# Layer 3's scales from bounds instead of measured maxima, in a four-layer graph kernel on one core

## What is computed

```python
v = causal_vars.at[:, intervention_idx].set(intervention_value)
for _ in range(MAX_STEPS):
    effects = jnp.einsum('nm,bmd->bnd', adj_matrix, v)
    h = jnp.concatenate([v, effects], axis=-1)
    h = jax.nn.relu(jnp.einsum('bnk,dk->bnd', h, W1) + b1)
    v = jnp.einsum('bnk,dk->bnd', h, W2) + b2
return v
```

## Time and profile before

| | us |
|---|---|
| three runs | 1045.5, 1045.57, 1046.95 |
| median | 1045.57 |
| the profiled execution's own time | 1046.92 |
| its span, first to last instruction | 1045.1 |
| PE busy in the span | 1024.1 |
| DVE busy | 692.9 |
| POOL busy | 534.7 |
| ACT busy | 453.1 |
| granted clock of TensorE, mean | 0.995 |

### The profile page before, as it was taken

How to read it: one execution, slowest core, us unless ns; L and a number is a source line. 1 busy time by engine, 2 the same in 40 slices (tenths; PEclk the granted TensorE clock), 3 DMA queues, 4 the chain that set the end, 5 groups by cost and what they waited for, 6 DMA issues and landing times.

```text
span 1045.1 us, 18762 instructions
## 1 busy us (share of the span) xinstructions
PE 1024.1 (98%) x6922; PEld 492.3 (47%) x6922; DVE 692.9 (66%) x1728; ACT 453.1 (43%) x1097; POOL 534.7 (51%) x625
## 2 busy tenths in 40 slices
PE   7999999999999999999999999999999999999995
PEld 3445444444444444434455555555554545455553
DVE  4877565656555886686577777875546676767556
ACT  4632323333334543444424667556557622141632
POOL 0005486644546686577645758579764233223311
PEclk9999999999999999999999999999999999999998
DMA  9930000000000000000010121112212100000022
GB/s 369 400 129 1 2 1 2 1 2 2 1 1 2 2 1 2 1 1 2 1 41 2 41 82 51 71 41 82 81 42 82 41 1 1 3 1 22 21 61 61
DMA packets 14658, 45.66 MB, mean 44 GB/s; under 512 B 960, under 2 KB 9280, under 8 KB 10080
## 3 DMA queue, kind: packets, MB, share of 16 engines
q1 hardware_dynamic: 14560, 44.39, 11.5%
HBM read 40.19 MB, written 4.19 MB: 42 GB/s over the span
## 4 chain that ended last, share of the span: by engine, by line
PE 95%; DVE 3%; ACT 1%; issue 0%; DMA 0%; SPq 0%; DVEq 0%; ACTq 0%
PE PS L771 37%; PE PS L901 23%; PE PS L945 18%; PE PS L823 5%; PE PS L756 2%; PE PS L758 2%; PE PS L757 2%; PE PS L765 1%; PE PS L764 1%; PE PS L763 1%; PE PS L746 1%; PE PS L926 1%; PE PS L747 1%; DVE X L1224 1%; DVE T L1224 0%; PE PS L809 0%
## 5 line engine op out<-in xcount | busy, mean ns | idle before, releaser
L771 PE MATMUL PS<-BW,S 128*128 128x512 fp8e4 x1792 | 403.2, 379 | 0.8 <-DVE R L1224 0.8
L771 PEld LDWEIGHTS PS<-BW,S 128*128 128x128 f16 x1792 | 169.9, 98 | 207.3 <-issue 16.6
L1064 ACT ACTIVATE T<-PS,SM 128x128 f32<-128x128 f32 x384 | 112.8, 365 | 234.5 <-DVE X L1224 157.2
L901 PE MATMUL PS<-WZ,R 64*128 64x512 f16 x1536 | 198.0, 377 | 1.7 <-ACT T L1064 1.7
L1768 POOL TENSOR_TENSOR T<-T 128x128 f32<-128x128 f32 (+1 forms) x192 | 124.3, 648 | 127.8 <-ACT T L1064 117.5
L1224 DVE SCALAR_TENSOR_TENSOR X<-PS,SM,X 128x128 f32<-128x128 f32 x320 | 110.0, 344 | 81.9 <-PE PS L901 81.9
L901 PEld LDWEIGHTS PS<-WZ,R 64*128 64x128 f16 x1536 | 69.5, 94 | 104.6 <-issue 26.3
L945 PE MATMUL PS<-BW,S 128*128 128x512 fp8e4 x512 | 115.4, 379 | 0.3 <-issue 0.3
L1224 DVE SCALAR_TENSOR_TENSOR T<-PS,SM,T 128x128 f32<-128x128 f32 x256 | 88.2, 344 | 28.9 <-PE PS L901 28.6
L1768 POOL TENSOR_TENSOR S<-R,S 128x512 f16<-128x512 f32 x48 | 57.5, 1210 | 93.5 <-ACT S L1064 93.5
L901 PE MATMUL PS<-WZ,T 64*128 64x512 f16 x768 | 103.8, 376 | 0.0
(11 more groups left out here) (215 smaller groups left out, 1480.0 us busy)
## 6 DMA issues: line engine op xcount, KB each, us to landing
WZ<-a_in SPq DMA_DIRECT2D x16, 1024.0 KB, 4.8
BW<-at_in SPq DMA_DIRECT2D x8, 1024.0 KB, 18.5
R<-at_in SPq DMA_DIRECT2D x7, 1024.0 KB, 12.4
out<-X SPq DMA_DIRECT2D x16, 256.0 KB, 2.3
X<-x_in SPq DMA_DIRECT2D x3, 1024.0 KB, 19.9
T<-w_in SPq DMA_DIRECT2D x1, 1536.0 KB, 15.4
R<-at_in SPq DMA_DIRECT2D x2, 512.0 KB, 4.8
SM<-sm_in SPq DMA_DIRECT2D x1, 520.5 KB, 18.0
```

What stands on the lines that cost most here:

```text
L771: m = e.matmul(o, stile(h, t, c), Bm[:, t, block(j)], start=(t == 0 and h == 0), stop=(last and t == NT - 1 and h == 1))
L901: m = e.matmul(bank(b0 + q), halves[kd][zh][r, :], WZ[r, wh, kd, block(g)], start=(i == 0), stop=(i == 8))
L1064: return e.activation(o, i, f, **kw)
```

## The change

The measured maxima go, with their semaphores and tiles. In `scales_b` the bound on the entries of pass 1's result is carried on to passes 2 and 3 by a factor `cNMG` (from column sums of the weights), and gives the scales of all three passes. The inverse, the scale and the factor `cKG` of each pass then stand there before layer 3 begins; `CR` becomes one row of 64 for each pass, written in step `rows`, and `rk` one row in place of two.

```diff
-    at(24, ("gmax", 1, 0))
-    at(25, ("gcol", 1, 0), ("step", 1, 0))
...
-        h, (p, g) = 14 * (n - 5), divmod(n - 2, 2)
-        on(h, ("gmax", p, g))
-        on(h + 2, ("gcol", p, g), ("step", p, g), *take(n, 0, "X11"))
+        h = 14 * (n - 5)
+        on(h + 2, *take(n, 0, "X11"))
...
-    for g in range(2):
-        on((29, 44)[g], ("fin", g))
+    on(29, ("fin",))
...
-        CR = flatR[:, 5248:5376].rearrange("p (k c) -> p k c", c=C)
-        rk = flatR[:, 5504:5536].rearrange("p (k t) -> p k t", t=NT)
+        CR = [flatR[:, k:k + C] for k in (5248, 5312, 5536)]
+        rk = flatR[:, 5504:5520]
...
-                elif kind == "gcol":
-                    p, g = step[1:]
-                    o = pe_aux(e, step)
-                    e.wait_ge(s_gmx, 2 * (p - 1) + g + 1)
-                    e.matmul(o[:, 0:128], gmh[:, g:g + 1].broadcast_to([128, 128]), i16[:, :], start=True,
-                             stop=True).then_inc(s_gmc, 1)
...
-                        fn(RT[k % 4], bank(product_bank(k)), ACT.Relu, scale=col(cKG0)).then_inc(s_gt, 1)
+                        fn(RT[k % 4], bank(product_bank(k)), ACT.Relu, scale=col(cKG + 1)).then_inc(s_gt, 1)
...
-                    p, g = divmod(n, 2)
+                    p = n // 2
                     e.wait_ge(s_p, slot_done(n, s, jj))
...
-                    e.wait_ge(s_kg, 2 * (p - 2) + g + 1)
                     o, i = RT[rt_buf(s, jj)], bank(pair_bank(n, s, jj))
                     if s == 6:
-                        fn(o, i, ACT.Relu, scale=col(cKG + g)).then_inc(s_gt, 1)
+                        fn(o, i, ACT.Relu, scale=col(cKG + p)).then_inc(s_gt, 1)
                     else:
-                        fn(o, i, ACT.Copy, scale=col(cKG + g)).then_inc(s_cp, 1)
+                        fn(o, i, ACT.Copy, scale=col(cKG + p)).then_inc(s_cp, 1)
...
-                    fn(RT[rt_buf(3, jj)], bank(aux_bank[step]), ACT.Copy, scale=col(cKG + n % 2)).then_inc(s_cp, 1)
+                    fn(RT[rt_buf(3, jj)], bank(aux_bank[step]), ACT.Copy, scale=col(cKG + n // 2)).then_inc(s_cp, 1)
...
-                fc(ts(e, col(cHB), col(cHB), 1e-10, qmax, ALU.max, ALU.mult))
-                fc(ts(e, col(cHB), col(cHB), 1.0 / 30000, None, ALU.mult))
-                fc(e.reciprocal(col(cT2), col(cHB)))
-                fc(ts(e, col(cKG0), col(cT2), col(cIRho), col(cT0), ALU.mult, ALU.mult))
-                fc(ts(e, cs[:, cSG:cSG + 4], ones[:, 0:4], col(cT2), None, ALU.mult))
-                fc(ts(e, cs[:, cISG:cISG + 4], ones[:, 0:4], col(cHB), None, ALU.mult))
+                fc(ts(e, col(cHB), col(cHB), 1e-10, None, ALU.max))
+                fc(e.tensor_tensor(col(cNMG), cs[:, cNG + 1:cNG + 2], cs[:, cNM + 1:cNM + 2], ALU.add))
+                fc(ts(e, col(cNMG), col(cNMG), 1e-3, None, ALU.max))
+
+                ip, sp, kp = ([col(k + p) for p in range(4)] for k in (cISG, cSG, cKG))
+                for p in (1, 2, 3):
+                    if p > 1:
+                        fc(stt(e, col(cHB), col(cHB), col(cNMG), col(cC1), ALU.mult, ALU.add))
+                    fc(ts(e, ip[p], col(cHB), qmax, 1.0 / (12000 if p < 3 else 60000), ALU.mult, ALU.mult))
+                    fc(e.reciprocal(sp[p], ip[p]))
+                    fc(ts(e, kp[p], sp[p], col(cIRho + min(p - 1, 1)), ip[p - 1] if p > 1 else col(cT0), ALU.mult, ALU.mult))
                 fc(e.tensor_copy(col(cFirst), col(cT1)))
```

`high`, its calls and the DVE side of `V` and `G`; the steps `gmax` and `step`, which go; `rows` and `fin`:

```diff
-            def high(f, c, j, n, largest):
-
-                hi = T[:, c, 0, block(j)]
-                ts(e, hi, f, 0.0, None, ALU.max).then_inc(s_gh, 1)
-                if largest:
-                    e.wait_ge(s_gh, n + 1)
-                    red(e, gm[:, c, j:j + 1], hi, ALU.max).then_inc(s_gm, 1)
+            def high(f, c, j):
+
+                ts(e, T[:, c, 0, block(j)], f, 0.0, None, ALU.max).then_inc(s_gh, 1)
...
-                        high(RT[k % 4], c, j, k - 16, True)
+                        high(RT[k % 4], c, j)
...
-                        stt(e, f, bank(pair_bank(n, s, jj)), cs[:, cKG + g:cKG + g + 1], f, ALU.mult, ALU.add).then_inc(s_ad, 1)
+                        stt(e, f, bank(pair_bank(n, s, jj)), col(cKG + p), f, ALU.mult, ALU.add).then_inc(s_ad, 1)
...
-                    high(f, c, j, place(p, c, j), p == 2)
+                    high(f, c, j)
...
-                                CR[:, c // 2:c // 2 + 1, :].broadcast_to([128, 2, C]), ALU.mult, ALU.add)
+                                CR[p - 1].unsqueeze(1).broadcast_to([128, 2, C]), ALU.mult, ALU.add)
...
-                elif kind == "gmax":
-                    p, g = step[1:]
-                    e.wait_ge(s_gm, 16 * (p - 1) + 8 * g + 8)
-                    red(e, gmh[:, g:g + 1], gm[:, 2 * g:2 * g + 2, :].rearrange("p c j -> p (c j)"), ALU.max).then_inc(s_gmx, 1)
-                elif kind == "step":
-                    p, g = step[1:]
-                    sG, iG = cs[:, cSG + g:cSG + g + 1], cs[:, cISG + g:cISG + g + 1]
-                    n = 2 * (p - 1) + g + 1
-                    e.wait_ge(s_gmc, n)
-                    red(e, gmr[:, g:g + 1], bank(aux_bank["gcol", p, g])[:, 0:128], ALU.max).then_inc(s_gmr, 1)
-                    e.wait_ge(s_gmr, n)
-                    fc(e.tensor_tensor(col(cT0), gmr[:, g:g + 1], iG, ALU.mult))
-                    fc(e.tensor_tensor(col(cT1), col(cT0), col(cIQ), ALU.mult))
-                    fc(ts(e, col(cT1), col(cT1), col(cNG + 1), col(cC1), ALU.mult, ALU.add))
-                    fc(ts(e, col(cT1), col(cT1), fr[:, 1:2], None, ALU.mult))
-                    fc(stt(e, col(cT0), col(cT0), col(cNM + 1), col(cT1), ALU.mult, ALU.add))
-                    fc(ts(e, col(cT0), col(cT0), 1e-10, 1.0 / 15000, ALU.max, ALU.mult))
-                    fc(ts(e, CR[:, g, :], c1row[:, :], sG, col(cRho + 1), ALU.mult, ALU.mult))
-                    fc(e.reciprocal(sG, col(cT0)))
-                    fc(ts(e, cs[:, cKG + g:cKG + g + 1], sG, iG, col(cIRho + 1), ALU.mult, ALU.mult))
-                    e.tensor_copy(iG, col(cT0)).then_inc(s_kg, 1)
-                    e.wait_ge(s_kg, n)
...
-                    fc(ts(e, CR[:, :, :], rows[:, 3:4, :].broadcast_to([128, 2, C]), col(cRho), col(cFirst), ALU.mult, ALU.mult))
+                    fc(ts(e, CR[0], rows[:, 3, :], col(cRho), col(cFirst), ALU.mult, ALU.mult))
+                    for p in (2, 3):
+                        fc(ts(e, CR[p - 1], c1row[:, :], col(cSG + p - 1), col(cRho + 1), ALU.mult, ALU.mult))
...
-                    g = step[1]
-                    fc(ts(e, rk[:, g, :], rmax, cs[:, cISG + g:cISG + g + 1], col(cFin), ALU.mult, ALU.mult))
+                    fc(ts(e, rk, rmax, col(cISG + 3), col(cFin), ALU.mult, ALU.mult))
```

More of the change, by code:

```diff
@@ L24 @@
 DV = 5
-(cZ, cW2, cWL, cTot, cQmax, cNQmin, cX, cQmin, cV0, cSV, cKG0, cIV, cC0, cC1, cT0, cT1, cT2, cT3, cCW, cFin,
+(cZ, cW2, cWL, cTot, cQmax, cNQmin, cX, cQmin, cV0, cSV, cNMG, cIV, cC0, cC1, cT0, cT1, cT2, cT3, cCW, cFin,
  cEz, cIQ, cHB, cFirst) = range(24)
@@ L324, in gnn_kernel @@
         xm = sb("xm", [128, NT], F32)
-        gm = sb("gm", [128, NC, 4], F16)
-        gmh = sb("gmh", [128, 2], F16)
-        gmr = sb("gmr", [128, 2], F32)
         wst = sb("wst", [128, 2], F32)
@@ L370, in gnn_kernel @@
         s_g, s_ut, s_uh, s_ul = (sem(f"s_{k}") for k in ("g", "ut", "uh", "ul"))
-        s_gt, s_gh, s_gl, s_gm, s_gmx, s_gmc, s_gmr, s_kg = (
-            sem(f"s_{k}") for k in ("gt", "gh", "gl", "gm", "gmx", "gmc", "gmr", "kg"))
+        s_gt, s_gh, s_gl = (sem(f"s_{k}") for k in ("gt", "gh", "gl"))
         s_f, s_y3 = sem("s_f"), sem("s_y3")
@@ L602, in take_banks @@
                         done = (s_ut, GN[step[1:]] + 1)
-                    elif kind == "gcol":
-                        done = (s_gmr, 2 * (step[1] - 1) + step[2] + 1)
                     elif kind == "total":
@@ L1688, in vector_steps @@
                         v = X[:, t, chunk(c)]
-                        m = stt(e, v, ps[:, 128 * i:128 * i + 128], rk[:, c // 2, t:t + 1], v, ALU.mult, ALU.add)
+                        m = stt(e, v, ps[:, 128 * i:128 * i + 128], rk[:, t:t + 1], v, ALU.mult, ALU.add)
                     m.then_inc(s_y3, 1)
@@ L1887, in slow_entry @@
             e.wait_ge(s_gt, 16 + 4)
-            for done in (s_gm, s_gl):
-                e.wait_ge(done, 32)
+            e.wait_ge(s_gl, 32)
             e.wait_ge(s_ul, len([x for x in CN if x in BEFORE]))
```

## The result

The changed kernel takes **1050.24 us** (median of 8 runs, 1048.06 to 1051.56) beside 1045.86 us of the kernel before on the same chip (8 runs, 1045.48 to 1046.95). The ratio is 1.0038, with a 95% interval from 1.0026 to 1.0049: slower by 4.4 us, where 1045.3 was forecast. Six of its later runs, on another chip, have a median of 1048.69 beside 1046.15 (ratio 1.0029, 1.0017 to 1.0041). All 16 times of it lie in two groups, seven from 1047.89 to 1048.38 at a mean granted clock of 0.996 or 0.997, and nine from 1049.36 to 1051.56 at 0.992 to 0.995.

What follows compares the result with a forecast made beforehand. PE was taken to bound the kernel, busy 485.72 of 486.00 us from 536 to 1022. Only four column matmuls counted, -0.22 us, all else 0: 1045.57 - 0.22 = 1045.35, so 1045.3 us; range 1044.5 to 1047.0.

Steps and rivals of the forecast that it cites:

- The low and the high end of the range: 1044.5 and 1047.0 us; each allowed 0.28 us at the branch, the low end also 0.5 in the end chain.
- code of another length may place otherwise: The 0.28 us of PE idle at the branch, taken off the low end and added to the high end.
- Rival C: First `G` of pass 3: a bank's new reader makes PE wait 2 or 4.1 us, up to 1049.5; chance 0.04.
- any other slip of banks or code: Catch-all for a slower result, included in the 0.04 chance of a PE wait on a bank's new reader.
- Rivals B and D: B: DVE work was on the path, below 1043.5, chance 0.05. D: work not taken away, no chance of its own.
- The end's wait: PE's wait at L756 in the last twenty microseconds, 2.4 us, forecast to stay near that.
- the reduces: 32 reduces into `gm` on DVE, 22.1 us busy, 0.689 each; removal costed at 0, hidden beside PE's products.
- the column matmuls: Four `gcol` matmuls removed from PE, 0.055 us each by distance of starts, 0.22 us gained.
- 6918 matmuls: PE's count forecast for the new profile, four matmuls fewer.
- 659: DVE's busy time forecast in us: 692.9 less 36, plus 2.
- the eight added operations: In the scales ahead of layer 3 on DVE, 0.23 us each, 1.8 us more; costed at 0.
- a cover of 11.6: Spare us before PE needs the low half of layer 2's unit 1, which follows the scales' chain on DVE.

Runs made afterwards that it cites:

- x12: Kernel before with each of the 32 128 x 512 reduces behind a high half done twice on VectorE: 1045.77 us beside 1045.58, ratio 1.0002.
- x1: Changed kernel with 9 never executed instructions added to PE's program, moving the code behind the branch: 1044.96 us beside 1045.64, ratio 0.9993.
- x9: Changed kernel with the fast path directly behind the branch on every engine but SyncE, which keeps the old order: 1045.92 us beside 1045.58, ratio 1.0002.
- x10: Kernel before with the fast path directly behind the branch and SyncE in the old order: 1046.13 us.
- x8: Changed kernel with flag inverted and the branch's two sides exchanged on every engine, fast path directly behind the branch: 1047.94 us, ratio 1.002.
- x2: Kernel before with 247 never executed instructions added to PE's program: 1050.62 us, ratio 1.005.
- x3: Changed kernel with 128 never executed instructions added: 1045.48 us, ratio 1.0.
- x11: Kernel before with each of four column matmuls issued 21 times, plus 136 never executed increments: 1049.85 us beside 1045.58, ratio 1.0047.
- x7: Changed kernel without the branch, all engines going straight into the fast path, exact path left out: 1045.36 us beside 1046.15, ratio 0.9994.
- x14: Changed kernel unedited, run again for its trace, the second such look: 1047.97 us.
- x6: Changed kernel unedited, run beside the others on another chip: 1048.69 us, median of 6 runs.
- x13: Changed kernel unedited, run once more for its trace: 1050.99 us.

## Why the prediction was wrong

*The step that failed* is the one on the branch. The low and the high end of the range took the 0.28 us of idle time there as all that "code of another length may place otherwise". That priced a jump by what was left uncovered in one layout, and not by what it takes: 3.6 us of the sequencer's time, hidden behind queued matmuls, and a second fetch behind it, hidden because the destination stood at the start of a piece. The removal of nine instructions ahead of the branch was known; the range should have had room for a stall of TensorE in which neither cost is covered. By the traces that stall cost 2.9 us more than the 0.28 allowed, and in part of the executions the clock 1.4 to 2.8 on top, which the sum had no term for.

*Rival C* ended on the right side with the wrong mechanism, and that its 1049.5 us lies near what was measured is luck. No bank's wait appeared: the two relus of the earlier trace rows start at 845.18 and 849.28 us now, and PE waits for no engine between 730 and 930 us. It gave "any other slip of banks or code" a share of 0.04 without a price of its own.

*Rivals B and D* got what they were given. The end's wait is 2.4 us still, the reduces are gone, and x12 shows that they lay beside TensorE's work.

*Right:* the column matmuls (0.053 us each measured, 0.055 said); 6918 matmuls; DVE at 658.3 us, where 659 was forecast; the eight added operations. The same operation of 1.03 us starts at 538.37 now, and the low half behind the chain at 545.43: 7.06 us, where it was 5.19, so 1.87 against the 1.8 said, under a cover of 11.6.

```profile
538.37 1.03 DVE L1378 TENSOR_TENSOR cs<-cs 128x1 f32<-128x1 f32 x1
...
545.43 0.69 DVE L1207 SCALAR_TENSOR_TENSOR T<-PS,T 128x512 f16<-128x512 f32 x1
```

*What no run can tell:* whether the change gains its 0.22 us. In the same place of the code (x1) it is 0.7 us below the kernel before, with an interval that includes no change at all; with the branch out of play (x9 against x10) it is 0.2 us below, within the scatter.

## What to carry to other kernels

In this kernel a branch over a long piece of code cost TensorE a fetch, and the place of its destination could cost it the wait for a second one; any edit that changes the number of instructions ahead of that destination, executed or not, rolls these dice again. So, where a kernel with a branch changes by a few microseconds and no engine waits for another, compare the waits on issue at the destination first, and pad code that is never executed before believing a verdict on the edit. And price a hidden cost by what it takes, not by the part that shows: the cover may be what your edit moves. A stall on the bounding engine is to be costed with the clock that it may lose behind it.

## What the runs showed of the hardware

- A branch that jumps over the exact path takes TensorE's sequencer 3.3 to 3.9 us (x1 3341 ns, the changed kernel 3814), one whose destination is directly behind it 83 ns (x8).
- TensorE's instructions came in pieces of 16 KB, which x2, x3 and x11 fit with 256 instructions each; the piece behind the destination's was asked for only once the destination was reached (909.4 us in the changed kernel), and where the destination stood near its piece's end TensorE could go on 3.04 to 3.33 us after its first matmul there (x14, x6). In straight code no border of a piece showed in TensorE's waits (x7).
- SyncE's jump at the end took 2.4 us to the next instruction (x8), with nothing to cover it; without the jump it was 0.2 us (x9).
- An idle time of 2.66 us was followed by the full clock (x14) and one of 2.67 by 5.7 us of products at the lower level (x13), in two executions of one program. Elsewhere 2.38 us of waiting for ACT were followed by a clock of 0.50 (x3, from 126 to 128 us), and 2.33 us at the same step (L901) by 1.00 (x10).
